# Bias attention with q, k and v projected once, and fp32 probabilities weighed in four column groups

## What is computed

```python
q, k, v = split(group_norm(x) @ w_qkv)          # 4 heads of 32 dimensions each
rw = rel_logits_1d(q, pos_emb_w)                # depends on the query and the key's column
rh = rel_logits_1d(q.transposed, pos_emb_h)     # depends on the query and the key's row
logits = q @ k.T / sqrt(32) + rw + rh           # n x n for each image and head
att = softmax(logits) @ v
```

## Time and profile before

| what | us |
|---|---|
| median of 3 runs | 8997.17 |
| lowest and highest run | 8979.13, 8999.67 |
| span of the profiled execution | 8991.1 |
| bias attention, from the first exponential (L816) to the last store (L567) | 141.6 to 2987.2 |

### The profile page before, as it was taken

How to read it: one execution, slowest core, us unless ns; L and a number is a source line. 1 busy time by engine, 2 the same in 40 slices (tenths; PEclk the granted TensorE clock), 3 DMA queues, 4 the chain that set the end, 5 groups by cost and what they waited for, 6 DMA issues and landing times. The chain is left out here.

```text
span 8991.1 us, 134766 instructions
## 1 busy us (share of the span) xinstructions
PE 8183.8 (91%) x42040; PEld 6708.4 (75%) x42040; DVE 6972.0 (78%) x7887; ACT 5713.1 (64%) x14778; POOL 6774.9 (75%) x3597
## 2 busy tenths in 40 slices
PE   6999999999999675999999999967999988888798
PEld 5777777777778334888888888845877868888775
DVE  6777777777777466999999999965777737999634
ACT  4877878878778346777777777712665614544304
POOL 3987978979879247999999999910877806999605
PEclk9999999999999876999999999978999989988898
DMA  2111111111111256444444444452000010000000
GB/s 97 29 47 29 47 48 28 48 44 32 47 28 38 108 202 210 106 106 108 104 107 107 106 108 104 110 224 94 22 26 16 24 48 20 1 1 1 20 8 20
DMA packets 480217, 600.84 MB, mean 67 GB/s; under 512 B 273736, under 2 KB 294480, under 8 KB 471568
## 3 DMA queue, kind: packets, MB, share of 16 engines
q1 hardware_dynamic: 478480, 591.31, 23.0%
q10 hardware_dynamic: 1024, 1.05, 0.1%
HBM read 349.14 MB, written 157.03 MB: 56 GB/s over the span
## 5 line engine op out<-in xcount | busy, mean ns | idle before, releaser
L865 POOL TENSOR_TENSOR l_probs_low<-l_probs,l_probs_high 128x512 fp32r<-128x512 f32 x1792 | 2424.7, 1388 | 514.0 <-ACT l_probs_high L818 505.5
L1601 POOL TENSOR_TENSOR m_c_h<-m_h,m_c 128x2048 f32<-128x2048 f32 x520 | 2341.9, 4589 | 44.4 <-DVE m_h L1588 44.3
L1588 DVE TENSOR_TENSOR_SCAN m_h<-m_decay,m_ps_x 128x1024 f32<-128x1024 f32 x1040 | 2273.3, 2263 | 89.5 <-issue 57.3
L1501 PE MATMUL m_ps_y<-m_c_h,m_ident 128*128 128x256 f32 x8320 | 1983.0, 381 | 2.1 <-POOL m_c_h L1601 2.1
L923 DVE TENSOR_REDUCE l_max_by_row<-l_ps_all 128x8 f32<-128x512 f32 x2048 | 1366.1, 685 | 438.6 <-PE l_ps_all L652 399.5
L1501 PEld LDWEIGHTS m_ps_y<-m_c_h,m_ident 128*128 128x128 f32 x8320 | 1513.8, 191 | 175.1 <-POOL m_c_h L1601 5.1
L816 ACT ACTIVATE l_probs<-l_ps_all 128x512 f32<-128x512 f32 x2048 | 1233.2, 602 | 329.8 <-PE l_ps_all L694 237.2
L818 ACT ACTIVATE l_probs_high<-l_ps_all 128x512 fp32r<-128x512 f32 x2048 | 1225.3, 598 | 0.0
L2615 POOL TENSOR_TENSOR s_late<-s_late,s_products 128x1024 f32<-128x1024 f32 x352 | 858.4, 2479 | 321.5 <-ACT s_products L2597 321.5
L2155 POOL TENSOR_TENSOR l_probs_low<-l_probs,l_probs_high 128x512 fp32r<-128x512 f32 x512 | 664.8, 1305 | 573.5 <-ACT l_probs_high L2138 559.2
L1525 ACT ACTIVATE m_b_diagonals<-m_steps,m_b_rows 128x32 fp32r<-128x32 f32 x4160 | 966.8, 306 | 3.3 <-DMA m_b_rows<-b_t 3.0
(11 more groups left out here) (383 smaller groups left out, 13774.2 us busy)
## 6 DMA issues: line engine op xcount, KB each, us to landing
m_delta_u<-du_t SPq DMA_DIRECT2D x1040, 128.0 KB, 3.6
m_c<-c_windows SPq DMA_DIRECT2D x130, 512.0 KB, 4.3
l_q_and_row_bias<-l_q_parts SPq DMA_DIRECT2D x64, 512.0 KB, 5.0
du_t<-m_delta_u_high SPq DMA_DIRECT2D x128, 256.0 KB, 3.0
du_t<-m_delta_u_low SPq DMA_DIRECT2D x128, 256.0 KB, 3.0
ys<-m_y SPq DMA_DIRECT2D x256, 126.0 KB, 4.8
m_direction<-ys SPq DMA_DIRECT2D x12, 2048.0 KB, 13.9
l_xn<-xn SPq DMA_DIRECT2D x8, 2048.0 KB, 10.9
```

What stands on the lines that cost most here:

```text
L865: pool.tensor_tensor(pl[:, slot, :], pt[:, slot, :], f(ph[:, slot, :]), ALU.subtract).then_inc(low_pool, 1)
L1501: ins = pe.matmul(y_ps[:, group % 2, 0:DIRS * SPAN].rearrange("p (d t) -> p d t", d=DIRS), ident[:, :], ch[:, group % CH, :, n, :], start= ...
L1588: dve.tensor_tensor_scan(h[:, u % H, :], decay[:, pair % 2, ct, k % 2, :, :].rearrange("p n t -> p (n t)"), x_ps[:, u % X, :], 0.0, ALU.mu ...
L1601: pool.tensor_tensor(ch[:, group % CH, 2 * pair % DIRS:2 * pair % DIRS + 2, :, :].rearrange("p d n t -> p d (n t)"), h[:, 2 * pair % H:2 * ...
```

## The change

Four things change, all in the first layer.

1. `group_norm` of this layer becomes `group_norm_and_project`. It projects q, k and v of all heads from the normalised map, and stores q and k in high and low parts and v by heads and tokens: 21 MB to DRAM in place of 4.2.
2. The tables `km`, `k2`, `qm` and `vv` get two slots. SP loads those of the next head (`load_tables`, ten DMAs) at row 1 of this one. The products on the embedding tables are issued at fixed tiles of the last two rows (`COLUMN_AT`, `ROW_AT`). Maximum units run on across the boundary of a head.
3. One exponential of each tile, in fp32. Tiles are taken in groups of three (`EACH`; the last has two). GpSimd adds up the three tiles of probabilities (`added`). TensorE weighs each tile with v as 32 fp32 stationary columns, the first into partitions 0 to 31 of the output bank, the next into 32 to 63 and 64 to 95, and the added tile with ones into 96 to 127.
4. At the end of a row ScalarE copies the one output bank (`empty`), and an fp32 product with a stacked unit matrix (`fold`) adds the three parts.

The order changes with it: `turn_bias` comes at tile 16 in place of 4, four transposes in place of four products; `turn` at 20 with 64 stationary columns.

```diff
@@ group_norm_and_project: sync @@
+                for kind, dst in enumerate((q_parts, k_parts)):
+                    sp.dma_start(dst[:, :, cols].rearrange("a p t -> p a t"), parts[:, c % RING, kind, :, :].bitcast(F32)).then_inc(stored[c % RING], 16)
...
@@ tensor @@
+                    if kind < 2:
+                        ins = pe.matmul(bank, w[:, kind * P:(kind + 1) * P], xo[:, cols], start=True, stop=True)
+                    else:
+                        for k in range(TW // P):
+                            tok = c * TW + k * P
+                            ins = pe.matmul(bank[:, k * P:(k + 1) * P], xo[:, tok:tok + P], w[:, 2 * P:3 * P], start=True, stop=True)
...
@@ bias_attention @@
-    SLOTS, LAG = 8, 3
+    EACH = 3
+    GATHERED = -(-KT // EACH)
+    SLOTS, SUM_SLOTS, LAG = 9, 3, 3
+    EARLY, EARLY_OF_HEAD, READY = 12, 6, 18
+    COPY_AT, INVERT_AT, FOLD_AT, DIVIDE_AT = 4, 12, 17, 19
+    TURN_BIAS_AT, MAXIMA_AT, TURN_AT, LOW_AT = 16, 18, 20, 23
+    COLUMN_AT, COLUMN_BANK = (6, 7, 9, 11, 12, 14, 20, 21), (7, 6, 7, 6, 7, 6, 3, 4)
+    ROW_AT, ROW_BANK = (1, 2, 4, 5, 7, 8, 10, 11), (7, 6, 7, 6, 7, 6, 7, 6)
...
+            def load_tables(it):
+                b, h, k = it // HEADS, it % HEADS, it % 2
+                tokens, rows = slice(b * L, (b + 1) * L), slice(h * D, (h + 1) * D)
+                if it >= 2:
+                    sp.wait_ge(scored, (it - 1) * NTB * KT)
+                    sp.wait_ge(weighed, weighed_at((it - 1) * NTB - 1, GATHERED - 1))
+                if it >= 1:
+                    sp.wait_ge(filled, it * 2 * NTB)
+                for first, part in ((0, 0), (D, 0), (SIDE, 1), (SIDE + D, 1)):
+                    sp.dma_start(f(qc[first:first + D, :]), q_parts[part, rows, tokens]).then_inc(qc_in, 16)
+                for dst, src in ((qm[0:D, k, :], q_parts[0]), (qm[D:2 * D, k, :], q_parts[1]),
+                                 (km[0:D, k, :], k_parts[0]), (km[D:2 * D, k, :], k_parts[0]), (k2[0:D, k, :], k_parts[1])):
+                    sp.dma_start(f(dst), src[rows, tokens]).then_inc(tables_in, 16)
+                sp.dma_start(vv[:, k, :, :], v_heads[it].rearrange("p (k d) -> p k d", d=D)).then_inc(tables_in, 16)
...
+            for row in range(ROWS):
+                if row + 1 < ROWS:
+                    copy_common(row + 1)
+                if row >= 1:
+                    send_sums(row - 1)
+                    spread_inverses(row - 1)
+                    store(row - 1)
+                if j == 1 and it + 1 < ITS:
+                    load_tables(it + 1)
+                if row + 1 < ROWS:
+                    copy_rows(row + 1)
...
-                pe.matmul(o, vv[:, i, :], ph[:, i % SLOTS, :], start=(i == 0), stop=False)
-                pe.matmul(o, vv[:, i, :], pl[:, i % SLOTS, :], start=False, stop=(i == KT - 1)).then_inc(weighed, 1)
+            def weigh(row, n):
+                it, tiles = row // NTB, tiles_of(n)
+                pe.wait_ge(pooled, pooled_at(row, n))
+                if n == 0 and row:
+                    pe.wait_ge(emptied, row)
+                for k, i in enumerate(tiles):
+                    o = ps[k * D:(k + 1) * D, OUT, :]
+                    last = i + EACH >= KT
+                    pe.matmul(o, vv[:, it % 2, i, :], pt[:, (row * KT + i) % SLOTS, :], start=(n == 0), stop=last)
+                o = ps[EACH * D:(EACH + 1) * D, OUT, :]
+                pe.matmul(o, ones[:, :], added[:, (row * GATHERED + n) % SUM_SLOTS, :], start=(n == 0), stop=(n == GATHERED - 1)).then_inc(weighed, 1)
...
+                pe.matmul(ps[0:D, FOLD, :], fold[:, :], weighed_sb[:, :], start=True, stop=True).then_inc(folded, 1)
...
+                    beside_column(row, i)
+                    beside_row(row, i)
+                    if row:
+                        weighings(row - 1, KT + i)
+                    weighings(row, i)
+                    if i == FOLD_AT and row:
+                        fold_up(row - 1)
...
@@ scalar @@
-                act.activation(pt[:, i % SLOTS, :], ps[:, i % 3, :], ACT.Exp)
-                act.wait_ge(weighed, weighed_at(row, i - SLOTS))
-                act.activation(ph[:, i % SLOTS, :], ps[:, i % 3, :], ACT.Exp).then_inc(expd, 1)
+                act.activation(pt[:, n % SLOTS, :], ps[:, n % 3, :], ACT.Exp).then_inc(expd, 1)
...
@@ gpsimd @@
-                        pool.tensor_tensor(pl[:, slot, :], pt[:, slot, :], f(ph[:, slot, :]), ALU.subtract).then_inc(low_pool, 1)
+                    for k, i in enumerate(tiles[1:]):
+                        tile = row * KT + i
+                        pool.wait_ge(expd, tile + 1)
+                        if k:
+                            pool.wait_ge(pooled, n)
+                        before = total if k else pt[:, (tile - 1) % SLOTS, :]
+                        pool.tensor_tensor(total, before, pt[:, tile % SLOTS, :], ALU.add).then_inc(pooled, 1)
```

More of the change, by code:

```diff
@@ L401, in bias_attention @@
+def bias_attention(nc, stage, q_parts, k_parts, v_heads, att, emb_h, emb_w, cells_in, ident_in, fold_in, sums, inverses):
+    HEADS, D = 4, 32
     QT, KC = TW // P, L // TW
@@ L418, in bias_attention @@
-    jobs = [(kind, t) for _, kind, t in plan]
-    number = {job: n for n, job in enumerate(jobs)}
-    place = [3 + t % 2 if kind == "q" else (3, 4, 7)[n % 3] if tile < 13 else (5, 7)[n % 2] for n, (tile, kind, t) in enumerate(plan)]
-    for kind, t, bank in (("k", 5, 7), ("v", 0, 5), ("v", 1, 5)):
-        place[number[kind, t]] = bank
-    before = [max((k for k in range(n) if place[k] == place[n]), default=None) for n in range(len(plan))]
-    JOBS, SPLITS = len(jobs), sum(kind != "h" for kind, _ in jobs)
@@ new lines, in bias_attention, with early, units @@
+    QL_LOADS, COMMON_LOADS, TABLE_LOADS = 16 * 2 * GROUPS, 16 * 2, 16 * 6
+    def early(row):
+        return EARLY if row % NTB else EARLY_OF_HEAD
+    def units(row, i):
+        part = []
+        if row + 1 < ROWS:
+            done = early(row + 1)
+            to_do = UNITS - done
+            part += [(row + 1, done + u) for u in range(to_do) if (u * READY + to_do // 2) // to_do == i]
+        if row + 2 < ROWS and i >= KT - early(row + 2):
+            part.append((row + 2, i - (KT - early(row + 2))))
+        return part
@@ new lines, in weighings @@
+            def weighings(row, i):
+                for n in range(GATHERED):
+                    if tiles_of(n)[-1] + LAG == i:
+                        weigh(row, n)
+            banks = (7, 6, 3, 4)
+            for t in range(NTB):
+                if t >= 4:
+                    column_split(0, t - 4)
+                column_job(0, t, banks[t % 4])
+            for t in range(NTB):
+                if t < 4:
+                    column_split(0, t + 4)
+                else:
+                    row_copied(0, t - 4)
+                row_job(t, banks[t % 4])
@@ new lines, in _ @@
+            row_copied(0, NTB - 1)
+            for u in range(UNITS):
+                max_unit(0, u)
+            turn_bias(0)
+            turn(0)
+            for u in range(early(1)):
+                max_unit(1, u)
+            pe.wait_ge(cells_placed, 2)
+            for i in range(2):
+                score(0, i)
+            for row in range(ROWS):
+                for i in range(KT):
+                    for block_of, u in units(row, i):
+                        max_unit(block_of, u)
+                    if row + 1 < ROWS:
+                        if i == TURN_BIAS_AT:
+                            turn_bias(row + 1)
+                        if i == TURN_AT:
@@ L775, in _ @@
-            for i in range(-KT, KT):
-                begin(0, 0, i)
-                for part in range(3):
-                    first_units(0, 0, i, part)
-            start(0, 0)
-            for it in range(ITS):
-                for j in range(NTB):
-                    attend(it, j, max(0, j + 3 - NTB) if it + 1 < ITS else 0)
+                        score(row, i + 2)
+                    elif row + 1 < ROWS:
+                        score(row + 1, i + 2 - KT)
+                    beside_column(row, i)
@@ new lines, in _ @@
+            dve.memset(ones[:, :], 1.0).then_inc(parts_ok, 1)
+            dve.wait_ge(const, 16 * 5)
+            for raw, parts in ((raw_eh, eh), (raw_ew, ew)):
+                chain.link(dve.tensor_copy(parts[:, :], raw[:, :]))
+                for first in (D, 3 * D):
+                    rows = slice(first, first + D)
+                    dve.tensor_tensor(parts[rows, :], raw[rows, :], f(parts[rows, :]), ALU.subtract).then_inc(parts_ok, 1)
+            banks = (7, 6, 3, 4)
+            for t in range(NTB):
+                split_column(0, t, banks[t % 4])
```

822 lines of the change are left out of this document (382 added, 440 removed).

## The result

The changed kernel took 8869.03 us (median of 4 runs, 8864.76 to 8869.82). The kernel before, on the same chip, took 8988.15 (4 runs, 8975.9 to 8999.67). The ratio is 0.9866 with a 95% interval of 0.9851 to 0.9882: 119 us or 1.3% faster, where 362 us were forecast. The time lies 19 us above the range's upper end. The profiled execution took 8869.04 us with a span of 8867.2, so 124 us less than the span of before.

What follows compares the result with a forecast made beforehand. TensorE was taken to bound the kernel, at 39.20 us a row with GpSimd 1.1 behind. Rows save 160 us, head boundaries 202, the start 0: 362 off 8997.17 gives 8635 us, range 8440 to 8850.

Steps and rivals of the forecast that it cites:

- Four groups at once: Weighing on TensorE: four products in four column groups run together, so a group costs 0.865 us and 11 cost 9.5.
- rival (a): Weighing groups do not run beside each other: 9243 us two at a time, 10,408 one by one; chance 0.12.
- the 32 records after the idle stretch: Earlier trace of L2338: 32 records in 1.95 us, read as four products at once from a standstill, no slower beginning.
- (c): Weighing: packing worth three, not four, as short groups fill and empty the array; group 1.15 us, 8839 us; chance 0.13.
- The end of a head: Head boundary: products on the embedding tables 8.4 us, plus some 3 us for the chain through bank, ScalarE and VectorE.
- The fold and the two turns: TensorE, each row: summing three partial outputs costs 0.9 us; turn_bias and turn keep 1.8 of 2.1 us.
- (b): GpSimd becomes the bound, its additions waiting; at 1.8 us each a row takes 38 to 39 us, 8795 us; chance 0.10.
- Splitting and joining, 11 x 0.2 = 2.2 us: TensorE, each row: each of 11 groups splits the array and joins it again, 0.2 us each, between 0 and 0.3.
- VectorE stays near 25 us. They cost nothing.: Ordinary row: VectorE near 25 us, and the other engines cost nothing while TensorE has 36.7 us of work.
- I put 6 us of stall, between 0 and 20: Head boundary: next head's table loads, 5.2 MB in 13 to 19 us, delay the row parts queued behind them.
- rival (d): Next head's table loads starve the row parts 20 us and more at each boundary: +100 us, 8735; chance 0.10.
- The start, "I count 0, between -15 and +25": Before the first row: projection ends near 72 us, first exponential at about 140 us against 141.6, so no net change.

Runs made afterwards that it cites:

- experiment 5: Changed kernel with groups weighed two at a time and the maxima's reduction reading 32 of 64 keys of each row: 8754.57 us, row 36.9 us.
- Experiment 3: Changed kernel with VectorE's reduction of the maxima reading only the first 32 of 64 keys of each row: 8815.58 us, row 38.15 us instead of 38.93.
- 4: Changed kernel with groups weighed two at a time, so the array is split 6 times a row in place of 11: 8827.25 us, row 37.8 us.
- Experiments 1: Changed kernel with SP issuing the next row's parts before the ten table loads instead of behind them: 8816.59 us, ratio 0.9808 to the kernel before.
- 2: Changed kernel with the ten table loads issued by ScalarE after tile 18 instead of by SP: 8826.89 us, ratio 0.9816 to the kernel before.
- 8: Changed kernel with the ten table loads issued two at a time over five rows, behind each row's parts: 8715.47 us, ratio 0.9703 to the kernel before.
- experiment 7: Changed kernel with GpSimd's casts of the cell tables held until VectorE's small subtractions are done: 8857.77 us, first copy at 205.02 instead of 214.05.

## Why the prediction was wrong, step by step

**The steps that held.** Four groups at once: 0.45 us between the bunches, and a row 27.2 us longer when they are serial, 27.7 forecast. So rival (a) was wrong, and the sign right. One reading behind it was wrong as it stands: the 32 records after the idle stretch in the earlier trace rows are (1.95 - 0.27) / 32 = 0.053 us each and not 0.029, so they did show a slower beginning, which the forecast and its case against (c) denied. The granted clock there was 0.50, and with half the clock 0.053 is again four at once; the forecast didn't look at it. A tile of score and maxima at 0.232 us a product stands. The end of a head is 10.8 us for 11.4. The fold and the two turns took what was put for them. GpSimd needs 1.28 to 1.30 us for an addition and 27.3 for a row; (b) was wrong. ScalarE at 20 us was right too.

**Splitting and joining, 11 x 0.2 = 2.2 us.** The term was there and too small: 0.33 us a group in the rows above, beyond the bound of 0.3, or +1.4 us a row. Its neighbours, and the earlier trace rows, gave 0.1 to 0.2. They have streams of 64 and 128 moving columns and not 512; whether that makes the difference no run shows. Pairing gives back 0.22 to 0.25 for each way in and out, and in experiment 5 the rest went into a new wait for VectorE, 0.4 us a row. Rival (c) had put a group's extra at 0.29 over the forecast; measured is 0.13, and not by its mechanism, as the bunches are no slower. The Trainium skill's rule ("TensorEngine Tiling (Array Packing)", Key Properties) that a change of mode drains the array fits the trace, in which the change costs 0.33 us.

**"VectorE stays near 25 us. They cost nothing."** The busy time was right (26.0) and the conclusion wrong. The forecast held an engine's sum over a row against TensorE's sum. The change makes the tiles unequal: with five products in every tile TensorE needed 1.16 us and a reduction of 0.69 fitted; now eleven tiles of 32 carry a group and the others are 0.70 us long. There VectorE sets the pace. Experiment 3 prices it at 0.75 us a row, with paired groups (experiment 5 against 4) at 0.9. This is the step that failed in its mechanism: a wait that the sum put at nothing. Together with 1.4 us of splitting it is all of the 2.2 us by which a row was missed.

**"I put 6 us of stall, between 0 and 20."** 19.7 us, at the very end of the range, and this was rival (d), priced at 8735 by itself. The mechanism was named; what was mis-sized is the rate. The ends for 5.2 MB were 13 and 19 us, from the earlier trace rows; it took 27 (576.6 to 604). Nine of the ten loads write 32 partitions each; that this is the reason is likely but not shown (see the last section). And the clock that falls during the stall was not counted. Experiments 1, 2 and 8 show that it is the burst that costs: moved behind one transfer it hits the next, and spread it costs nothing. So (d) came true, but on top of a missed row and a late start. The range's upper end added such terms up to 195 us; they were 262.

**The start, "I count 0, between -15 and +25".** +30 by the first copy. Two sizes and one overlap failed. The stage of the projection ends 14.6 us late: its stores run at some 350 GB/s and not 419, which makes 60 us of 50, and the first is issued at 22.70, some 6 us after the 16.9 from which the forecast counted. GpSimd's casts hold VectorE up, 9 us by experiment 7, where the forecast let them overlap. The rest, some 7 us, fits the loads of the first head: in experiment 7 the first table product waits for them until 106.99, 20.7 us after their stage begins at 86.29, and 13 us were put for all of them (for the 8 MB that the forecast names this would be over 600 GB/s). No run prices this by itself. The forecast's own list, from 72 on, also adds up to 133 us and not to the "about 140" it gives.

**The sum.** The forecast let its three unknown costs meet only at the range's end. All three came out dear, at 135 + 96 + 30 us. Two of the three bounds were passed (0.3 us a group and +25 at the start), the third was reached (20 us of stall), and VectorE's pace had no bound at all. That the measured time still lies only 19 us outside is partly luck: the end of the heads, the last two rows and the later stages gave back 21 us. The lower end was also added up wrongly: without a stall 7 x 6 = 42 us go, not 60, and 8635 - 141 - 42 - 15 is 8437; with the 60 it would be 8419 and not 8430. Nothing hangs on it here.

## What to carry to other kernels

Compare two engines tile by tile and not row by row once the tiles become unequal: an engine with a third of its time free can still set the pace in the light tiles. Look for it in the waits of the weight loads, since a wait between two products can be counted as busy; but price it by a run with a lighter engine, since most of such a wait may be covered (here 90.7 us of waiting were worth some 10). A background load of some megabytes should be cut up over the time that it has; reordering a burst only picks which small transfer is late. Products that use part of the array are best issued in long batches, as each batch pays its way in and out.

## What the hardware showed that was not expected

- Casts on GpSimd hold up small VectorE operations on SBUF: a subtraction of 32x127 took 3.6 us instead of 0.3 and a cast of 128x127 took 3.51 instead of 0.23, each until just after a cast of GpSimd's ended. The Trainium skill ("GPSIMD Engine Reference", Specifications) says that the two share their SBUF interfaces and contend when VectorE has two SBUF inputs or works in a 2-port mode. The trace agrees for the subtraction, which has two inputs; which mode the cast works in no run shows.
- Ten loads of 512 KB, nine of them into 32 partitions each, moved at about 200 GB/s; the 2 MB of the earlier trace rows into 128 partitions reached 419. At the start of the changed kernel the same ten loads follow a load of 2 MB into 128 partitions in the same queue, also of 16 KB a partition: the DMA view from 86 to 126 us has 360 to 459 GB/s for that and 180 to 262 for most of the time behind it. No run changed the partitions alone.
- A 2 KB store behind them took up to 19.5 us, and issuing the burst from another engine gave back only a third of the stall.
- Going to 32 stationary columns and back costs 0.33 us with streams of 512 columns by the starts in the trace, and 0.22 to 0.25 us of it come back when such a change is saved. The way in is the same 0.32 us from product to product whether four groups work or one.
